# A graph network's edge pass: two of three low-part subtractions move from GpSimd to VectorE

## The reference

```python
# layer 0, per edge message m, aggregated by dst
m  = concatenate([h[dst], h[src]]) @ W_pre.T + b_pre
mx, mn = segment_max(m, dst), segment_min(m, dst)      # 0 where a node has no edge
mean = segment_sum(m, dst) / deg
std  = sqrt(relu(segment_sum(m * m, dst) / deg - mean * mean) + 1e-5)
agg  = concatenate([mx, mn, mean, std])
scaled = concatenate([agg, agg * log(deg + 1), agg / log(deg + 1)])
x = x + (concatenate([h, scaled]) @ W_post.T + b_post) @ W_lin.T + b_lin
# layer 1
h = relu(layernorm(x)); agg = segment_sum(edge_attr, dst) / max(count, 1)
x = x + relu(concatenate([h, agg]) @ W1 + b1) @ W2 + b2
```

## Time and profile before

| | |
|---|---|
| median of three runs | 1666.87 us (1665.56 to 1671.47) |
| the profiled execution, its own time | 1669.48 us |
| its span, first to last instruction | 1667.7 us |
| mean granted TensorE clock | 0.965 of 2.4 GHz |
| node pass, roughly | up to 590 us |
| edge pass, roughly | 590 to 1660 us |
| chunks of edges | 49 |

### The profile page before, as it was taken

How to read it: one execution, slowest core, us unless ns; L and a number is a source line. 1 busy time by engine, 2 the same in 40 slices (tenths; PEclk the granted TensorE clock), 3 DMA queues, 4 the chain that set the end, 5 groups by cost and what they waited for, 6 DMA issues and landing times.

```text
span 1667.7 us, 33188 instructions
## 1 busy us (share of the span) xinstructions
PE 1520.5 (91%) x8747; PEld 1268.2 (76%) x8747; DVE 1306.2 (78%) x4229; ACT 930.2 (56%) x1976; POOL 1293.9 (78%) x1379
## 2 busy tenths in 40 slices
PE   2899999999999589999989999999999989999995
PEld 2789999999999468777777777777777777777783
DVE  5899999999999488777776677777777766777781
ACT  1799999999999334444434444444443444443441
POOL 1777777777778787888888888888888888888753
PEclk9799999999999889999999999999999999999998
DMA  3455555555555522233222233333233323333200
GB/s 85 163 208 206 205 205 203 201 201 202 204 204 190 171 86 83 82 85 82 85 78 80 82 89 88 90 91 87 87 89 81 83 85 91 91 91 92 82 20 17
DMA packets 158897, 197.94 MB, mean 119 GB/s; under 512 B 18912, under 2 KB 115321, under 8 KB 158858
## 3 DMA queue, kind: packets, MB, share of 16 engines
q1 hardware_dynamic: 136906, 149.93, 27.7%
q0 software_dynamic: 21952, 47.55, 9.5%
HBM read 111.11 MB, written 90.17 MB: 121 GB/s over the span
## 4 chain that ended last, share of the span: by engine, by line
PE 43%; POOL 27%; issue 16%; DVE 8%; ACT 2%; another core or an unknown queue 2%; POOLq 1%; DMA 1%; SPq 0%; DVEq 0%; ACTq 0%
PE bank L571 12%; POOL y L474 6%; PE bank L580 5%; POOL rows L461 5%; POOL agg_lo L400 5%; POOL hs L461 5%; PE bank L592 3%; PE bank L590 3%; PE bank L591 3%; PE bank L554 3%; PE bank L562 3%; PE bank L620 2%; POOL attr_mean L486 2%; POOL xdc L413 2%; PE bank L617 2%
## 5 line engine op out<-in xcount | busy, mean ns | idle before, releaser
L617 PE MATMUL bank<-comb_hi,agg_lo 128*128 128x384 f32 x588 | 212.6, 362 | 67.7 <-POOL agg_lo L400 64.8
L461 POOL DMA_INDIRECT hs<-table,idx x196 | 202.6, 1034 | 59.7 <-issue 56.9
L461 POOL DMA_INDIRECT rows<-table,idx x196 | 200.5, 1023 | 59.7 <-issue 59.7
L613 PE MATMUL bank<-comb_lo,agg_hi 128*128 128x384 f32 x588 | 230.5, 392 | 16.5 <-DVE nout L983 12.6
L474 POOL DMA_INDIRECT y<-nout,oidx x196 | 196.1, 1001 | 54.8 <-issue 51.6
L379 POOL TENSOR_TENSOR runs<-nx,b_all 128x512 f32<-128x512 f32 x98 | 125.6, 1282 | 109.0 <-DVE nx L993 108.9
L571 PE MATMUL bank<-w_sb,nut 128*128 128x128 f32 x1568 | 201.5, 282 | 3.9 <-ACT nut L780 2.8
L614 PE MATMUL bank<-comb_hi,agg_hi 128*128 128x384 f32 x588 | 201.1, 342 | 0.0
L571 PEld LDWEIGHTS bank<-w_sb,nut 128*128 128x128 f32 x1568 | 183.4, 192 | 22.5 <-issue 11.8
L617 PEld LDWEIGHTS bank<-comb_hi,agg_lo 128*128 128x128 f32 x588 | 112.9, 192 | 92.9 <-POOL agg_lo L400 86.6
L620 PE MATMUL bank<-comb_sd,agg_sd 128*128 128x384 f32 x392 | 170.4, 518 | 0.0
(11 more groups left out here) (180 smaller groups left out, 4159.4 us busy)
## 6 DMA issues: line engine op xcount, KB each, us to landing
table<-rows SPq DMA_DIRECT2D x98, 512.0 KB, 2.7
rows<-in_x SPq DMA_DIRECT2D x98, 256.0 KB, 3.1
y<-nout SPq DMA_DIRECT2D x98, 256.0 KB
inv<-inv_row SPq DMA_DIRECT2D x49, 256.0 KB
attr<-in_edge_attr SPq DMA_DIRECT2D x48, 256.0 KB
keep<-keep_row SPq DMA_DIRECT2D x49, 128.0 KB
reset<-reset_row SPq DMA_DIRECT2D x49, 128.0 KB
lift<-lift_row SPq DMA_DIRECT2D x49, 128.0 KB
```

Of the source, the lines that this page charges most:

```text
L461: pool.indirect_dma_start(out=to[:, s, j, :], out_offset=None, in_=of, in_offset=bass.IndirectOffsetOnAxis(ap=idx[:, s, which, j:j + 1], a ...
L613: pe.matmul(acc[:, 0:SCALERS * P], hi, w_lo, start=(a == MX), stop=False, skip_group_check=True)
L617: pe.matmul(acc[:, 0:SCALERS * P], lo, w_hi, start=False, stop=False, skip_group_check=True)
```

## The change

GpSimd's `low_part` and its four calls go. VectorE's `low_part`, there for the mean already, is called for MX and MN too, directly ahead of the mean, and takes over the wait on `e_layer0` that protects the two buffers of `agg_lo`. The operands, the number of subtractions, the semaphores and the order of maximum, minimum and mean stay as they are, and so does all that TensorE and ScalarE do.

```diff
@@ gpsimd @@
-            def low_part(a, rows, c, i):
-
-                pool.wait_ge(sem(f"e_hi{a}"), c + 1 + EU * i)
-                if c >= 2:
-                    pool.wait_ge(sem("e_layer0"), TILES * (c - 1) + TILES * EU * i)
-                pool.tensor_tensor(agg_lo[:, c % 2, a, :], rows[:, c % 2, :], agg_hi[:, c % 2, a, :],
-                                   ALU.subtract).then_inc(sem(f"e_lo{a}"), 1)
-
             def edge_step(k, i):
...
-                if k == -1:
-
-                    low_part(MX, run_max, 0, i)
-                    low_part(MN, run_min, 0, i)
...
-                c = k + 1
-                if edge(c) and k >= 0:
-                    low_part(MX, run_max, c, i)
-                    low_part(MN, run_min, c, i)
                 c = k - 2
                 if edge(c):
@@ vector @@
             def low_part(a, rows, c, i):

                 dve.wait_ge(sem(f"e_hi{a}"), c + 1 + EU * i)
+                if c >= 2:
+                    dve.wait_ge(sem("e_layer0"), TILES * (c - 1) + TILES * EU * i)
                 dve.tensor_tensor(agg_lo[:, c % 2, a, :], rows, agg_hi[:, c % 2, a, :],
                                   ALU.subtract).then_inc(sem(f"e_lo{a}"), 1)
...
                 if have:
                     mix_amp(k, 2, i)
                 if ahead:
+                    low_part(MX, run_max[:, b, :], c, i)
+                    low_part(MN, run_min[:, b, :], c, i)
                     low_part(ME, mean_b[:], k + 1, i)
                 if have:
                     mix_att(k, 2, i)
```

## The result

The changed kernel took 1646.48 us against 1668.13 us of the kernel before on the same chip: a ratio of 0.986, 95% interval 0.9845 to 0.9875, so 1.4% faster. The prediction was 1574 us, range 1549 to 1612: a gain was right, 92 us of it forecast, 22 us came. The profiled execution took 1645.29 us.

The account below looks back on a forecast made before the run. GpSimd was taken to bound the edge pass: its step falling from 21.92 to 19.91 us saves 84.4 us over 42 steps, with 4 us ahead and 4 behind, together 92 us: 1574 us, range 1549 to 1612.

Parts of the forecast that it names:

- GpSimd as the bound of the kernel before: Edge pass: GpSimd, waiting for nobody, sets the pace at 21.92 us a step; TensorE could go 2.8 us a chunk faster.
- Taken off GpSimd: Between last gather and first scatter: two subtractions and their joints go, 2.38 us a step.
- contention: VectorE's two new subtractions slow GpSimd's transfers by 0.37 us a step, bounds 0 and 1.38.
- my bound of 19.54: GpSimd's step after the removal, 21.92 - 2.38 us, with no added loss from VectorE's new operations.
- its rate of 0.27 us per us: GpSimd's loss per microsecond of VectorE's two-operand SBUF work beside the gathers, applied to 1.38 us of new work.
- Added on VectorE: Two subtractions of 0.69 us each fit the 1.70 us idle ahead of the mean's low part: no cost.
- Who is late next: GpSimd at 19.91 us a step stays slower than TensorE at 19.14, so it remains the bound.
- no price of its own: Signals of finished matmuls seemed held back at TensorE's L617 wait, delaying ScalarE and VectorE; no separate cost assigned.
- New waits of TensorE for `attr_mean`: At L696, behind GpSimd's last operation in a step: a few tenths of a us a chunk in the later half.
- the signs that I had named for being wrong: GpSimd idle beyond issue gaps, gathers growing over 0.1 us each, or TensorE waiting for VectorE's mixed tiles.
- the four rivals: TensorE's pace, 0.17; contention up to full length, 0.19; no shorter step, 0.05; slower through VectorE's chain, 0.07.
- Rival 1: TensorE becomes the bound at 19.14 us a chunk: 116 us less, 1551 us in all; chance 0.17.

Follow-up runs that it names:

- low parts last: The kernel before with GpSimd's two low parts moved from between gathers and scatters to behind the scatters; 1665.6 us, ratio 0.999 to the kernel before.
- group 3: Kernels run on one chip; here the changed kernel with GpSimd's `attr_mean` put between gathers and scatters: 1540.1 us, 0.925 of the kernel before.
- group 5: Later runs on one chip; here the changed kernel with GpSimd's `attr_mean` put between gathers and scatters: 1570.0 us, 0.943 of the kernel before.
- `attr_mean` moved: The changed kernel with GpSimd's `attr_mean` moved from behind the scatters to between gathers and scatters; 0.925, 0.946 and 0.943 of the kernel before.
- the added-only kernel: The kernel before, GpSimd keeping its low parts, with the same two subtractions also made on VectorE into an unread buffer; 1685.3 us, ratio 1.0105.
- the break: The changed kernel with one tiny GpSimd operation between the last gather and the first scatter; 1759.8 us, against 1752.4 for the changed kernel beside it.
- the earlier place: The changed kernel with GpSimd's `attr_mean` moved ahead of the gathers; 1723.3 us, ratio 1.027 to the kernel before.

## Why the prediction was wrong

*GpSimd as the bound of the kernel before*: right. Without late signals and with the same work (low parts last) its step was 21.77 us and the time 1665.6 us.

*Taken off GpSimd, 2.38 us, and contention, 0.37 us, a step of 19.91 us*: right in size, in part by luck. Where GpSimd waited for hardly anybody, with late signals about, it took 19.94 and 19.67 us. In group 3 its step was 19.15 us, below my bound of 19.54. GpSimd's groups from 700 to 1400 us (busy, mean ns) say why, of group 3 first, then of group 5:

```profile
L449 POOL DMA_INDIRECT rows<-table,idx x146 | 154.4, 1058 | 44.5 <-issue 44.5
L468 POOL DMA_INDIRECT y<-nout,oidx x148 | 148.1, 1001 | 40.0 <-issue 40.0
L449 POOL DMA_INDIRECT hs<-table,idx x146 | 145.5, 997 | 50.1 <-issue 50.1
...
L445 POOL TENSOR_TENSOR gather_go<-eps_col 128x1 f32<-128x1 f32 x36 | 6.9, 193 | 2.9
```
```profile
L449 POOL DMA_INDIRECT rows<-table,idx x144 | 165.0, 1146 | 43.9 <-issue 43.9
L468 POOL DMA_INDIRECT y<-nout,oidx x141 | 152.3, 1080 | 38.1 <-issue 38.1
L449 POOL DMA_INDIRECT hs<-table,idx x143 | 136.9, 957 | 49.0 <-issue 49.0
```

`gather_go` fell from 0.61 us on average to 0.19, since it no longer runs beside VectorE's scan of squares: 0.42 us that the bound of 19.54 had left in, so 19.12. The prediction had counted these 0.42 us as a loss that stays and grows. The twelve transfers took 4 x (1.058 + 1.001 + 0.997) = 12.22 us in group 3 and 12.73 in group 5, which is all but 0.01 us of the 0.52 between the two steps; before they took 12.23. So contention with the transfers, 0.37 us in the prediction, came to nothing in group 3, to 0.50 us in group 5 and to 0.33 us where the addition was tried alone: its rate of 0.27 us per us is no constant, it goes with what happens to coincide.

*Added on VectorE, nothing*: right where signals are on time (1.44 us in the gap). In the changed kernel's profile the gap is not always there, and the mean's low part averages 0.98 us (the 43 of them from 660 to 1560 us) against 0.69. With the additions left out, though, the time got no better.

*Who is late next*: this step failed. It said that GpSimd at 19.91 us is slower than TensorE at 19.14 and stays the bound. It set against GpSimd only TensorE's own pace, taken from chunk 46, the one part of the trace that has no gathers. The prediction had seen signals of finished matmuls held back and gave that "no price of its own", without a reason. In the kernel before it had none: `hst` and `nout` waited 123.3 us at "remote", and the kernel with the same work and no such waits was no faster, since GpSimd's pace covered them. With GpSimd shorter, TensorE, VectorE and ScalarE waiting for each other through late signals take 21.38 us a step, and GpSimd, 19.65 us without its waits, waits for them. `nut` and `part` are the late readers now, which before were on time, so the trace of before had not shown what these would cost. The missing 1.47 us over 19.91, times 42, are 62 us of the 72 between forecast and result. Most of the rest lies behind chunk 46's `xdc`: from there to the end it took 103.1 us, where it took 97.7 before and I had set 4 less. New waits of TensorE for `attr_mean` (L696 before, L680 now) did not come either; GpSimd waits instead, and TensorE waits for mixed tiles (L597, 10.4 us in 25 waits), two of the signs that I had named for being wrong. None of the four rivals had this mechanism. That the late signals, and not something else in the changed kernel, are what holds it there is read from its trace and from the kernels without them; the changed kernel itself was never seen without them.

*Rival 1, TensorE's pace*, forecast 902 us for 47 chunks and 1551 us in all. With signals on time and `attr_mean` moved it was 901.52 us and 1540.1 us; most of the 11 us lies ahead of chunk 1, whose first matmul came at 589.5 us, 15 us earlier than in the kernel before.

What stays open. That late signals need the gathers is shown by when they start and end in 16 profiles and by the one run without gathers, on a chip that had them. That a kernel has gathers is not enough: the added-only kernel had gathers, such a chip and, in the execution that was profiled, no late signals. How a gather delays a signal of TensorE was not found; the order with `attr_mean` between reduces what they cost, in the two groups that had them, but neither the break nor the earlier place explains it. Why a chip or an execution has them was not found, nor what the changed kernel, unedited, would take where they are absent: its profile had them each of the three times. But for one wait, its VectorE and ScalarE programs are those of the kernel without scatters, in which TensorE was busy for all of 650 to 1440 us and which took 1529.5 us.

## What to carry to other kernels

Before an engine's work is cut, ask what its pace has been hiding: a wait that costs nothing now gets its price when the cover goes, and a row named "remote" with no cost is such a wait. A pace read from the stretch where a transfer has run out need not be the pace beside that transfer: here it was in one kernel (19.18 us a chunk against 19.14) and not in the other. Where a profile shows a delay that no instruction explains, run the same kernel at several times and on several chips before reading an order of operations into it: four kernels here looked free of late signals by their order, and the one that was run again had some of them. A loss of 0.04 us a step can be a loss and a gain of nearly ten times its size; look at the groups of instructions before calling a cost nothing.

## What the hardware showed

TensorE's signals can reach the other engines microseconds after the matmul that gives them (4.2 us above, while TensorE itself went on), here only from the first gather to 9 us behind the start of the last, in 16 of 20 profiles. One kernel took 1540.1, 1570.0 and 1587.2 us in three groups while the kernel before stood at 1666.0, 1665.3 and 1676.0. VectorE's subtraction of 0.68 us took 1.91 us beside GpSimd's own, and its four-element `ms` 3.07 us, while GpSimd's subtractions kept their 1.28 us. The twelve indirect transfers of a step took from 12.22 to 12.73 us with the same work on both engines (the changed order, groups 3 and 5). A stop of TensorE of 1.6 us was followed by a granted clock of 0.50 from 1132 to 1134 us.
